# Decoder layer with a routed expert stage on one core: routing and the shared expert's products of a software pipeline at a lag of three turns, and zero rows stored in 16 parts

## The reference, cut to what matters

```
scores = sigmoid(tokens @ router_weight.T)         # 32 experts in 4 groups
# the best 2 groups, in them the best 4 experts; weights normalised, times 2.5
mixed  = sum over the 4 chosen e of w[e] * (silu(t @ gate[e].T) * (t @ up[e].T)) @ down[e].T
shared = (silu(t @ shared_gate.T) * (t @ shared_up.T)) @ shared_down.T
out    = layernorm(x + mixed + shared)
```

## Time and profile before

| | |
|---|---|
| runs | 799.15, 801.12, 802.53 us; median 801.12 |
| profiled execution | 804.18 us, of it 802.40 span |
| TensorE matmul busy | 747.6 us (93%) |
| DVE, ACT, POOL busy | 564.9 (70%), 475.9 (59%), 350.2 us (44%) |
| mean granted TensorE clock | 0.967 |
| DMA issues | zero rows 4 x 1032 KB; experts' weights 16 x 768 KB; context 16 x 384 KB; xT and x 16 x 256 KB each; hs 16 x 256 KB |

### The profile page before, as it was taken

One profiled execution on the slowest core, in us unless ns is written; L12 is line 12 of the kernel. 1 busy time (PEld: TensorE's weight loads), 2 busy tenths in 40 slices (PEclk: granted clock), 3 DMA queues, 4 the chain that ended last, 5 costly groups with the idle time before them and its releaser, 6 DMA issues.

```text
span 802.4 us, 21736 instructions
## 1 busy us (share of the span) xinstructions
PE 747.6 (93%) x8276; PEld 631.1 (79%) x8276; DVE 564.9 (70%) x2038; ACT 475.9 (59%) x1110; POOL 350.2 (44%) x418
## 2 busy tenths in 40 slices
PE   8899989999999999999988775799999999999986
PEld 7777778888888888888877653688888888888554
DVE  4356558898889888988898864456666666664586
ACT  2666666777777766776674422456666666663133
POOL 0112103434553455335534753445555555555242
PEclk9999999999999999999999965989999999999999
DMA  7412151543633343333113424987777877772996
GB/s 255 149 53 71 61 140 55 187 144 110 193 124 107 100 133 120 112 106 123 68 42 107 133 107 136 365 269 238 240 240 258 275 259 241 244 235 87 387 402 244
DMA packets 73530, 138.83 MB, mean 173 GB/s; under 512 B 10449, under 2 KB 41681, under 8 KB 73170
## 3 DMA queue, kind: packets, MB, share of 16 engines
q1 hardware_dynamic: 56194, 97.97, 38.5%
q0 software_dynamic: 12864, 35.28, 11.9%
q10 hardware_dynamic: 4368, 4.20, 1.5%
HBM read 89.53 MB, written 47.87 MB: 171 GB/s over the span
## 4 chain that ended last, share of the span: by engine, by line
PE 81%; DVE 9%; DMA 5%; issue 2%; SPq 2%; ACT 1%; POOL 0%; ACTq 0%; DVEq 0%
PE banks L605 13%; PE banks L340 11%; PE banks L625 7%; PE banks L413 4%; PE banks L445 4%; PE banks L390 3%; PE banks L436 3%; PE banks L557 3%; PE banks L381 3%; PE banks L426 3%; PE banks L548 3%; PE banks L522 3%; PE banks L398 3%; PE banks L514 2%; PE banks L488 2%; PE banks L502 2%
## 5 line engine op out<-in xcount | busy, mean ns | idle before, releaser
L1410 POOL DMA_INDIRECT y<-yb_tile,idcol_tile x140 | 134.4, 960 | 113.2 <-DVE yb_tile L1258 108.9
L605 PE MATMUL banks<-xbT_tile,wgu_tile 128*128 128x128 f32 x1024 | 138.2, 279 | 0.0
L1258 DVE SCALAR_TENSOR_TENSOR yb_tile<-banks,rowsb_tile 128x256 f32<-128x256 f32 x140 | 67.6, 483 | 87.1 <-PE banks L625 52.6
L605 PEld LDWEIGHTS banks<-xbT_tile,wgu_tile 128*128 128x128 f32 x1024 | 127.4, 196 | 0.2 <-ACT xbT_tile L810 0.2
L949 ACT ACTIVATE wgu_tile<-w_expert_tile 128x512 f32 x128 | 79.8, 623 | 24.2 <-DVE tab_i_tile L1233 17.2
L1388 POOL DMA_INDIRECT routed<-row_tile,idx_tile x64 | 62.6, 978 | 66.3 <-PE banks L458 50.8
L625 PE MATMUL banks<-w_expert_tile,hb_tile 128*128 x256 | 78.6, 389 | 0.6 <-DVE hb_tile L1245 0.6
L937 ACT ACTIVATE gb_tile<-banks 128x128 f32<-128x128 f32 x140 | 38.9, 278 | 65.3 <-PE banks L605 58.7
L1382 POOL DMA_INDIRECT routed<-row_tile,idx_tile x64 | 61.7, 964 | 34.8 <-issue 18.5
L1363 POOL TENSOR_TENSOR rs_tile<-ve_tile,half_neg_tile 128x2 f32<-128x2 f32 x16 | 11.1, 695 | 145.1 <-DVE ve_tile L1052 145.1
L810 ACT ACTIVATE xbT_tile<-banks 128x256 f32<-128x256 f32 x140 | 52.9, 378 | 9.7 <-PE banks L340 7.5
(11 more groups left out here) (242 smaller groups left out, 1822.0 us busy)
## 6 DMA issues: line engine op xcount, KB each, us to landing
w_early_tile<-w_expert SPq DMA_DIRECT2D x48, 384.0 KB
rowsb_tile<-routed SPq DMA_DIRECT2D x128, 129.0 KB, 3.0
w_expert_tile<-y SPq DMA_DIRECT2D x15, 1024.0 KB, 15.6
w_expert_tile<-w_expert SPq DMA_DIRECT2D x16, 768.0 KB, 4.9
cT_tile<-ctxT SPq DMA_DIRECT2D x16, 384.0 KB, 3.1
routed<-zrow_tile SPq DMA_DIRECT2D x4, 1032.0 KB, 7.1
xT_tile<-xT SPq DMA_DIRECT2D x16, 256.0 KB, 3.0
x_sb_tile<-x SPq DMA_DIRECT2D x16, 256.0 KB, 2.8
```

Source lines behind the costliest of these rows:

```text
L605: m = e.matmul(o[:, h * P:(h + 1) * P], wgu[s % WG][:, k * D + h * EI:k * D + (h + 1) * EI], xbT[s % 2][:, k * P:(k + 1) * P], start=k == ...
L1258: e.scalar_tensor_tensor(yb[s % YS][:, :], bank[6 + s % 2][:, 0:D], rowsb[s % ROWS][:, D:D + 1], rowsb[s % ROWS][:, 0:D], ALU.mult, ALU.ad ...
L1410: e.indirect_dma_start(y, bass.IndirectOffsetOnAxis(ap=idcol[n % ROWS][:, :], axis=0), yb[n % YS][:, :], None).then_inc(SEM[f"st_y{n % YS} ...
```

## The change

The loop is one turn shorter on each engine (`nseq + 5`). x2T, router, gate, up, rank, and on ACT and DVE the helpers that go with them, work on sequence t - 3; the scatters on t - 4 and t - 5. For that norm2 runs at the start of ACT's turn, just behind z, on the sequence whose out2 ended the last turn, and rs2 is the first in POOL's turn. norm1 moves on ACT from ahead of sha to behind shb, and x1T gets a wait for it. up stands right behind gate. hs is stored at t - 4, with a semaphore for each of its two buffers. The zero rows are stored in 16 parts of 258 KB, in SP's turns 2 to 17, ahead of the context load.

```
 pe_z:      after(v_key, i - 4)                        -> i - 3
 pe_x1T:    + wait_ge(a_x1, i + 1)
 pe_av2:    after(v_h1, i - 1)                         -> i
 pe_x2T:    after(v_hs, i - 1)                         -> i
 pe_gate:   after(a_vo, min(i + 5, nseq))              -> i + 4
            - after(v_ve2, min(i + 2, nseq))
 pe_up:     - after(a_sc, min(i + 2, nseq)), after(v_hs, i)
            + wait_ge(a_sc, i + 1)
 act_gates: after(st_hs, 16 * (i - 1))                 -> after(st_hs{i % 2}, 16 * (i // 2))
 pool_scattera: after(p_s2, min(i + 4, nseq))          -> i + 3
 pool_scatterb: after(p_s2, min(i + 5, nseq))          -> i + 4

 @blk.tensor, for t in range(nseq + 6)                 -> nseq + 5
   scores2(t-2) x2T(t-4) z(t) router(t-4) vo(t) scores1(t) up(t-5) pTa(t-2) gate(t-4) v(t) ...
-> scores2(t-2) z(t) vo(t) x2T(t-3) scores1(t) router(t-3) pTa(t-2) gate(t-3) up(t-3) v(t) ...
   ... q(t-1) rank(t-4) out2(t-2)                      -> ... q(t-1) rank(t-3) out2(t-2)
 @blk.scalar
   x2T(t-4) z sc(t-4) norm1(t-1) sha vo tanh pTa shb pr gates(t-4) ... k norm2(t-3) q v
-> z norm2(t-3) sha x2T(t-3) vo tanh sc(t-3) pTa shb norm1(t-1) pr gates(t-3) ... k q v
 @blk.vector
   route, hs1, choice, key (t-4), hs2 (t-5)            -> all (t-3), same places
 @blk.gpsimd
   scatterb(t-6) scattera(t-5) xc(t) xc2(t-2) rs2(t-3) rs1(t)
-> rs2(t-3) scatterb(t-5) scattera(t-4) xc(t) xc2(t-2) rs1(t)
 @blk.sync
   xT(t) x(t) context(t) store_hs(t-6) load_rest(with zero rows for i in ZERO)
-> xT(t) x(t) store_zero(t-2) context(t) store_hs(t-4) load_rest
```

More of the change, by code:

```diff
@@ L377, in pe_z @@
             e.wait_ge(SEM["ld_xT"], 16 * (i + 1))
-            after(e, SEM["v_key"], i - 4)
+            after(e, SEM["v_key"], i - 3)
             for db in range(DK):
@@ L527, in pe_x2T @@
             e.wait_ge(SEM["a_x2"], i + 1)
-            after(e, SEM["v_hs"], i - 1)
+            after(e, SEM["v_hs"], i)
             for k in range(DK):
@@ L543, in pe_gate @@
         def pe_gate(e, i):
-            after(e, SEM["a_vo"], min(i + 5, nseq))
-            after(e, SEM["v_ve2"], min(i + 2, nseq))
+            after(e, SEM["a_vo"], min(i + 4, nseq))
             for b in range(DK):
@@ L552, in pe_up @@
         def pe_up(e, i):
-            after(e, SEM["a_sc"], min(i + 2, nseq))
-            after(e, SEM["v_hs"], i)
+            e.wait_ge(SEM["a_sc"], i + 1)
             for b in range(DK):
@@ L955, in _ @@
             e.wait_ge(SEM["v_setup"], 2)
-            for t in range(nseq + 6):
-                if live(t - 4):
-                    act_x2T(e, t - 4)
+            for t in range(nseq + 5):
                 if live(t):
                     act_z(e, t)
[L962 to L965, removed]
+                if live(t - 3):
+                    act_norm2(e, t - 3)
                 if live(t - 2):
                     act_sha(e, t - 2)
+                if live(t - 3):
+                    act_x2T(e, t - 3)
                 if live(t):
@@ L1394, in _ @@
             e.wait_ge(SEM["v_setup"], 4)
-            for t in range(nseq + 6):
-                if live(t - 6):
-                    pool_scatterb(e, t - 6)
+            for t in range(nseq + 5):
+                if live(t - 3):
+                    pool_rs2(e, t - 3)
                 if live(t - 5):
-                    pool_scattera(e, t - 5)
+                    pool_scatterb(e, t - 5)
+                if live(t - 4):
+                    pool_scattera(e, t - 4)
                 if live(t):
@@ L1514, in _ @@
                 if s == ROWS:
-                    e.wait_ge(SEM["st_hs"], 16 * nseq)
+                    for u in range(2):
+                        e.wait_ge(SEM[f"st_hs{u}"], 16 * nseq // 2)
                     e.dma_start(hs_sb[:, :, :, :].rearrange("p i k s -> p (i k s)"), inner[:, :]).then_inc(SEM["ld_hs"], 16)
```

90 lines of the change are left out of this document (44 added, 46 removed).

## The result

The kernel after takes **811.6 us** (median; 809.99 to 813.89), the kernel before, timed beside it, 801.8 us. The ratio is **1.011**, 95% interval 1.007 to 1.015: slower by 1.1%, where 800.5 and a range of 794 to 806 had been forecast. (Ratios are given as on record; they differ from the quotient of the medians by up to 0.002.) The profiled executions lie closer together: 809.99 us with a span of 808.2, against 804.18 and 802.4, so 5.8 us are to be found in the traces.

The account below looks back on a forecast made before the run. TensorE's own work was taken to bound turns 5 to 15, with gains only where it waits and in the drain. Terms +2.0 +1.4 +0.8 -1.1 +1.7 +1.0 +1.3 -7.7 sum to -0.6 us: median 800.5, range 794.0 to 806.0.

Parts of the forecast that it names:

- Full turns: Turns 5 to 15: TensorE waits for x2 in each of 11 turns, +2.0 us in sum.
- so each turn waits 0.18 us: Full turn: x2 is ready at 4.87 us, TensorE gets there at 4.69; bounds 0 and 0.4 a turn.
- Rival (b): Turns 3 to 17: DVE comes 0.6 us later to x2, chain bounds each turn, +9.0 us, 809.5; chance 0.15.
- so DVE comes early to it: Argument against a late x2: key waited for TensorE's rank in 15 turns, 11.6 us in all.
- The drain: Turns 16 and 17: up behind pTa +1.7 and +1.0 us, half clock +1.3 for both together.
- so pTa isn't later: Turn 16: the wait for x2 and the router fit into the 7.65 us before pTa.
- the first of the slow matmuls run in the shade of shb: Turns 16 and 17: half clock behind a 3.7 us gap is partly hidden; +1.3 us, bounds 0 and 4.
- The term for up: Turns 16 and 17: up no longer fills the gap and comes behind pTa, +1.7 and +1.0 us.
- Turn 2: x1T waits for norm1 behind shb, +1.4 us; zero rows and weights sent before spread, +0.8 us.
- Turns 3 and 4: TensorE's stops in spread, 1.35 and 2.78 us, put down to DMA bursts, both go: -1.1 us.
- rival (c): Turns 3 and 4: the stops aren't made by the burst and stay, +3.9 us in sum, 805.0; chance 0.10.
- The end: Turn 18 to the expert stage's first row load: 32.2 us where it was 39.97, -7.7 us.

Follow-up runs that it names:

- early_and_norm1: Kernel after with rank ahead of q, norm2 ahead of z, norm1 in its old place in turns 1 and 2, no filler: 802.1 us, ratio 0.998.
- change_once_more: Kernel after, unchanged, run again on the third chip beside the kernel before: 811.6 us against 803.8, ratio 1.012.
- all_fixes_again: Kernel after with rank ahead of q, norm2 ahead of z, old norm1 in turns 1 and 2, filler matmuls in turns 16 to 18: 798.1 us, ratio 0.994.
- fill_clock: Kernel after plus 7, 7 and 11 unused matmuls in turns 16, 17 and 18, between scores2 and x2T: 832.5 us, ratio 0.997.

## Why the prediction was wrong

**Full turns: the wait was right, its price wrong (+2.0 forecast, +4.7 measured).** The step that failed is "so each turn waits 0.18 us". The 0.17 us is there, but I took a wait to cost its own length. The transposes behind the wait take 0.22 us more on the chain than the same ones without it; I read that as the overlap with the matmuls ahead of them, which a wait takes away; no run shows that this is the cause. Another 0.09 us at pTa has no explanation in the traces. My upper bound of 0.4 a turn was for a longer wait, not for this. The rest of the chain (POOL at 3.79, x2 at 4.92) was right to 0.1 us, with some luck: the copy of z, left out, held norm2 up by 0.15 us, and norm2 was 0.09 shorter than charged.

**Rival (b)** named the place, the chain out2 - x2 - rs2 - norm2 - x2T, and its sign came true; its mechanism, a DVE that comes later to x2 than in the kernel before, did not: x2 begins 0.73 us into the turn in both. Key still waits for TensorE's rank, by the table of waits 10.9 us in 15 turns against the earlier trace rows:

```profile
DVE key_tile L1168 <- PE banks L563: 10.9, 15, 1.0
```

But the prediction's reading of this wait, "so DVE comes early to it", proves nothing for x2: behind the wait, DVE has key and the rows to make before it, and is late for x2 by those 0.73 us. The chain that bounds the turn begins at rank. That the swap of rank helped fits this; it was never run without that of norm2.

**The drain: the clock (+1.3 forecast with bounds 0 and 4).** The steps that failed are "so pTa isn't later" and "the first of the slow matmuls run in the shade of shb". They fill the shade and pass it: pTa 0.8 us late, gate 3.49 instead of 1.89, and the rest of the turn behind them. Keeping the clock at 1.00 was worth 45.7 - 41.9 = 3.8 us, near the upper bound. The other 2.2 us of the kernel after went with the earlier x2. The term for up, +1.7 and +1.0, was right by the chains (+1.7 and +1.2). That 2.85 us remain when wait and clock are mended fits it only by chance, since a stop of 1.32 us and an earlier start of DVE stand in it. The stop in turn 16 (0.95 us in the kernel after) was in no term; its cause stays open. The row that spoke for a small price, turns 16 and 17 almost wholly at full clock, was one of a kernel that had x2T and the router to fill that very gap.

**Turn 2 (+1.4 and +0.8 forecast, +1.9 measured).** norm1 behind shb cost 1.7 to 2.0 us by the two comparisons, the stop with it: 0.94 us with the wait at x1T, 0.19 without it in `early_and_norm1`. I had two causes for what goes away with one edit.

**Turns 3 and 4 (-1.1 forecast, +0.3 measured; 54.0 us, -0.6, in `change_once_more`, and 53.9 in the two kernels without the wait).** The stops shrank to 0.81 us together, and rival (c), that they stay, fell. These 0.81 and the two waits at their real price are what is missing. The cause I gave isn't shown: large parts of zeros with the new order brought no stop back. By the Trainium skill, "Runtime: NRT & Kernel Launch", "Instruction fetch mechanics", instruction fetch is hidden; the traces have stops of 0.3 to 4.2 us for which they name no semaphore, so if these are fetches, the rule doesn't hold here.

**The end (-7.7 forecast, -7.75 measured).** x2T, the first scatter of the last sequence and the first row load each came within 0.2 us. That the sum is exact is partly luck: the prediction let TensorE's chain set the first scatter (19.8) and had POOL "nearly as late" (19.5); it was POOL, at 19.7, and up had run at a better clock than charged (2.32 us, not 3.53). Right was its reason for counting nothing for the earlier tables: the last scatter held the row load. The end was also 32.0 and 31.8 us in the kernels with an earlier x2, so while POOL's 20 scatters stand in a row, a faster TensorE gains nothing there.

With the two sizes as measured (+4.7 for +2.0, +8.9 for +4.0) the sum would have been -0.6 + 2.7 + 4.9 = +7.0, 811.2 for the profiled execution, which took 810.0. The rest is the start, 1.5 us earlier for no reason of the change (turn 2 starts between 43.2 and 45.5 us in the profiles), the expert stage (-0.75) and turn 2 (-0.3), against turns 3 and 4 (+1.4).

## What to carry to other kernels

Moving a step into the iteration that has just made its input shortens the tail once and puts a chain of four engines into every full turn: price it per turn, and charge a wait on TensorE with more than its length (here, in one pair of kernels, a wait of 0.17 us cost 0.43). Follow the chain back past the engine that is busy: key's wait for rank looked like slack of DVE and was the head of the chain. Then take the wait away with what can go ahead of it; here two swaps of neighbours gave back 5 us, and with norm1 and a filler the change went from 1.2% slower to 0.6% faster. In a drain, ask what fills the gap in which TensorE waits, and let something run there if the work behind it is on the path.

## What the runs showed of the hardware

A gap of 3.8 us in turn 16 was followed by TensorE at half clock (router 1.92 us for 0.97), and filler matmuls in the same place held the granted clock at 1.00 in `all_fixes_again`: 7 matmuls in each that compute nothing made turns 16 and 17 shorter by 3.8 us together. Where TensorE still waited 0.62 us before x2T behind the filler (`fill_clock`; the wait of 1.1 us before the router is in both), the clock of turn 16 was 0.93, and the gain of both turns 1.4 us. The same gap of 3.8 us was followed by transposes at full clock in `change_once_more` (0.66 us, in the kernel after 1.12), and by the router at half clock in both.

One kernel took 802 to 835 us on different chips. The expert stage alone took 309 us on one and 318 on another (506.8 to 825.0 us in the second profile of before), and the waits put down to "issue" over the whole span rose from 0.3 to 50 us on DVE, and from 4.6 to 17.6 us on TensorE, between the first and the second profile of the kernel before. A change of 1% can have one sign on one chip and none on the next, so the two kernels belong on the same chip, and a verdict on more than one.
